# A top-1 mixture of low-rank experts: fp32 products taken directly instead of as three products of rounded parts, with TensorE's work per tile in another order

## What is computed

```python
h = h + _L0_ffn_ref(_layernorm(h, axis=-1), L0_ffn_route_w, L0_ffn_A, L0_ffn_Bw)

def _L0_ffn_ref(x, route_w, A, Bw):            # x (16, 128, 1024); A (8, 16, 1024); Bw (8, 1024, 16)
    logits = jnp.einsum('bsd,ed->bse', x, route_w)
    topk_v, topk_idx = jax.lax.top_k(logits, 1)
    route_weight = jax.nn.one_hot(topk_idx[..., 0], E, dtype=logits.dtype) * topk_v
    h = jnp.einsum('bsd,erd->bser', x, A)
    wh = route_weight[..., None] * h
    out = jnp.einsum('bser,eor->bso', wh, Bw) * SCALING
    return out
```

## Time and profile before

| what | value |
|---|---|
| median of 3 runs | 3199.29 us |
| the three runs | 3191.82, 12855.53 and 3199.29 us |
| span of the profiled execution | 3196.4 us |
| granted TensorE clock, mean over the span | 0.956 of full |
| PE busy | 2877.8 us, 90% of the span |
| DVE, ACT and POOL busy | 1687.9, 998.1 and 1014.7 us |

### The profile page before, as it was taken

One profiled execution on the slowest core, in us unless ns is written; L12 is line 12 of the kernel. 1 busy time (PEld: TensorE's weight loads), 2 busy tenths in 40 slices (PEclk: granted clock), 3 DMA queues, 4 the chain that ended last, 5 costly groups with the idle time before them and its releaser, 6 DMA issues. The chain is left out here.

```text
span 3196.4 us, 38209 instructions
## 1 busy us (share of the span) xinstructions
PE 2877.8 (90%) x13385; PEld 2335.5 (73%) x13385; DVE 1687.9 (53%) x2915; ACT 998.1 (31%) x2062; POOL 1014.7 (32%) x442
## 2 busy tenths in 40 slices
PE   6777499999989999998999999999999878649999
PEld 5555377777777777777777777777777667538888
DVE  5999654554544454455454446555444547662332
ACT  3443332333232333223332223333322323541111
POOL 3443233343333343333343333344333300141110
PEclk9999699999999999999999999999999979779999
DMA  4221032232222232222232222223222110110000
GB/s 93 47 49 40 28 93 73 74 95 74 78 66 73 72 94 78 76 75 66 67 92 85 72 74 72 66 86 92 72 72 72 60 53 1 40 60 27 27 26 27
DMA packets 55368, 206.90 MB, mean 65 GB/s; under 512 B 6880, under 2 KB 7136, under 8 KB 53216
## 3 DMA queue, kind: packets, MB, share of 16 engines
q1 hardware_dynamic: 55264, 205.52, 21.5%
HBM read 197.11 MB, written 8.39 MB: 64 GB/s over the span
## 5 line engine op out<-in xcount | busy, mean ns | idle before, releaser
L741 POOL TENSOR_TENSOR at_wlo<-at_wstage,at_whi 128x1024 fp32r<-128x1024 f32 x192 | 478.0, 2490 | 1374.9 <-ACT at_whi L764 1374.9
L1006 PE MATMUL at_proj<-qr_xhi,at_whi 128*128 128x512 f32 x1536 | 636.9, 415 | 57.5 <-POOL at_wlo L741 53.2
L1008 PE MATMUL at_proj<-qr_xhi,at_wlo 128*128 128x512 f32 x1536 | 612.4, 399 | 0.0
L1007 PE MATMUL at_proj<-qr_xlo,at_whi 128*128 128x512 f32 x1536 | 611.1, 398 | 0.0
L1006 PEld LDWEIGHTS at_proj<-qr_xhi,at_whi 128*128 128x128 f32 x1536 | 291.7, 190 | 135.0 <-issue 53.3
L1007 PEld LDWEIGHTS at_proj<-qr_xlo,at_whi 128*128 128x128 f32 x1536 | 291.6, 190 | 70.6 <-issue 7.4
L1008 PEld LDWEIGHTS at_proj<-qr_xhi,at_wlo 128*128 128x128 f32 x1536 | 290.9, 189 | 70.2
L733 POOL TENSOR_TENSOR at_wolo<-at_ostage,at_wohi 128x1024 fp32r<-128x1024 f32 x126 | 312.3, 2499 | 33.6 <-ACT at_wohi L770 33.5
L1054 PE MATMUL at_out<-at_wohi,at_ohi 128*128 128x512 f32 x1008 | 314.6, 394 | 9.0 <-DVE at_wolo L733 7.0
L1054 PE MATMUL at_out<-at_wohi,at_olo 128*128 128x512 f32 x1008 | 313.5, 393 | 0.0
L1054 PE MATMUL at_out<-at_wolo,at_ohi 128*128 128x512 f32 x1008 | 312.3, 391 | 0.0
(11 more groups left out here) (262 smaller groups left out, 4798.2 us busy)
## 6 DMA issues: line engine op xcount, KB each, us to landing
at_wstage<-in_w_qkv_dram SPq DMA_DIRECT2D x192, 512.0 KB, 3.6
at_ostage<-in_w_o_dram SPq DMA_DIRECT2D x128, 512.0 KB, 3.9
cv_x<-in_x_dram SPq DMA_DIRECT2D x32, 512.0 KB, 6.5
out_dram<-h SPq DMA_DIRECT2D x16, 512.0 KB, 2.6
fn_w_lo_raw<-in_w_t_dram SPq DMA_DIRECT2D x8, 512.0 KB, 7.0
fn_qka_lo_raw<-in_qka_t_dram SPq DMA_DIRECT2D x5, 512.0 KB, 5.9
sc_fhi_raw<-in_dft_fwd_dram SPq DMA_DIRECT2D x4, 512.0 KB, 7.4
sc_chi_raw<-in_lag_cos_dram SPq DMA_DIRECT2D x2, 512.0 KB, 9.7
```

What stands on the lines that cost most here:

```text
L741: pool.tensor_tensor(w_lo[j % 2][:, :], w_stage.buffers[j % 2][:, :], w_hi[j % 2][:, :].bitcast(F32), ALU.subtract).then_inc(wlo_done, 1)
L1006: pe.matmul(proj[:, j % 2, :], hi[:, w], x_hi[:, k, :], start=(k == 0), stop=False)
L1007: pe.matmul(proj[:, j % 2, :], hi[:, w], x_lo[:, k, :], start=False, stop=False)
L1008: last = pe.matmul(proj[:, j % 2, :], lo[:, w], x_hi[:, k, :], start=False, stop=(k == KT - 1))
```

## The change

In the mixture, and nowhere else:

- The rows `mx_x` and the weights `mx_ar`, `mx_b` and `mx_wt` stay plain fp32. The remainders are gone, with the operations on ACT and DVE that made the parts. Each projection block is one plain fp32 matmul instead of three fp32r ones (8 a tile instead of 24), and so is each output bank (2 instead of 6).
- `mx_ar` comes in one DMA of 1088 columns instead of 1024 and 64, and no operation follows it. PE waits for `mx_ar` and `mx_b` themselves.
- The transposed weighted values have two buffers `mx_wt0` and `mx_wt1`.
- PE's order in the turn of tile t is now: projections of t, transposes of t+1, outputs of t-1, transpose of `mx_wh` of t.

The core of the diff:

```diff
+    def copy(self, act, t, par, used, count):
+
+        after(act, self.turned, t + 1)
+        after(act, used, count)
+        act.copy(self.x[par][:, :, :], self.tp[:, :, :].rearrange("p a (k t) -> p (a k) t", t=P))\
+           .then_inc(self.hi_done, 1)
...
                 def before():
-                    ar.high(act)
                     rows.normalize(act, 0, 0)
-                    rows.high(act, 0, 0, pj_done, 0)
+                    rows.copy(act, 0, 0, pj_done, 0)
                     rows.normalize(act, 0, 1)
-                    b.high(act)
...
                     after(act, wt_mm, t + 1)
-                    after(act, out_mm, t)
-                    act.copy(wt_hi[:, :], wt[:, 0:P]).then_inc(wthi_done, 1)
+                    if not early(t, 2):
+                        after(act, out_mm, t - 1)
+                    act.copy(wt_sb[i % 2][:, :], wt[:, 0:P]).then_inc(wt_done, 1)
...
                 def body(g, i, t, on):
-                    if on(1):
-                        rows.low(dve, t + 1, (i + 1) % 2)
                     route_of(t)
                     if on(-1):
                         add(t - 1)
-                    after(dve, wthi_done, t + 1)
-                    dve.tensor_tensor(wt_lo[:, :], wt[:, 0:P], wt_hi[:, :].bitcast(F32), ALU.subtract)\
-                       .then_inc(wtlo_done, 1)
...
-                def outputs(t):
-                    after(pe, wtlo_done, t + 1)
+                def outputs(t, par):
+                    after(pe, wt_done, t + 1)
                     after(pe, added, t)
                     for c in range(2):
-                        w = slice(c * BANK, (c + 1) * BANK)
-                        pe.matmul(out[:, c, :], wt_hi[:, :], b.hi[:, w], start=True, stop=False)
-                        pe.matmul(out[:, c, :], wt_hi[:, :], b.lo[:, w], start=False, stop=False)
-                        mm = pe.matmul(out[:, c, :], wt_lo[:, :], b.hi[:, w], start=False, stop=True)
+                        mm = pe.matmul(out[:, c, :], wt_sb[par][:, :], b[:, c * BANK:(c + 1) * BANK],
+                                       start=True, stop=True)
                     mm.then_inc(out_mm, 1)
...
                 def body(g, i, t, on):
-                    after(pe, rows.lo_done, t + 1)
+                    after(pe, rows.hi_done, t + 1)
+                    after(pe, wh_done, t)
+                    for k in range(KT):
+                        mm = pe.matmul(pj[:, 0:ROUTED], rows.x[i % 2][:, k, :], ar[:, k * ROUTED:(k + 1) * ROUTED],
+                                       start=(k == 0), stop=(k == KT - 1))
+                    mm.then_inc(pj_done, 1)
                     if on(1):
                         rows.turn(pe, t + 1)
-
-                    after(pe, wh_done, t)
-                    xh, xl = rows.x_hi[i % 2], rows.x_lo[i % 2]
-                    for k in range(KT):
-                        w = slice(k * ROUTED, (k + 1) * ROUTED)
-                        pe.matmul(pj[:, 0:ROUTED], xh[:, k, :], ar.hi[:, w], start=(k == 0), stop=False)
-                        pe.matmul(pj[:, 0:ROUTED], xh[:, k, :], ar.lo[:, w], start=False, stop=False)
-                        mm = pe.matmul(pj[:, 0:ROUTED], xl[:, k, :], ar.hi[:, w], start=False, stop=(k == KT - 1))
-                    mm.then_inc(pj_done, 1)
                     if on(-1):
-                        outputs(t - 1)
+                        if early(t, 2):
+                            pe.wait_ge(b_in, 16)
+                        outputs(t - 1, (i + 1) % 2)
                     after(pe, wh_done, t + 1)
-                    after(pe, wtlo_done, t)
+                    after(pe, wt_done, t)
                     pe.transpose(wt[:, 0:P], wh[:, :], ident[:, :]).then_inc(wt_mm, 1)
```

More of the change, by code:

```diff
@@ L1105, with __init__ @@
     LINKS = 3 + RSQRT_LINKS + 1
-    def __init__(self, nc, ctx, name, h, ident):
+    def __init__(self, nc, ctx, name, h, ident, split=True):
         def sb(n, shape, dt=F32):
@@ L1115, in __init__ @@
         self.xn = sb("xn", [P, L])
-        self.x_hi = [sb(f"xhi{i}", [P, KT, P], F32R) for i in range(2)]
-        self.x_lo = [sb(f"xlo{i}", [P, KT, P], F32R) for i in range(2)]
+        if split:
+            self.x_hi = [sb(f"xhi{i}", [P, KT, P], F32R) for i in range(2)]
+            self.x_lo = [sb(f"xlo{i}", [P, KT, P], F32R) for i in range(2)]
+        else:
+            self.x = [sb(f"x{i}", [P, KT, P]) for i in range(2)]
         self.st = sb("st", [P, GROUP, 2, 6])
@@ L1206, in __init__ @@
     def __init__(self, nc, ctx, name, h, ident, rstd, shift):
-        super().__init__(nc, ctx, name, h, ident)
+        super().__init__(nc, ctx, name, h, ident, split=False)
         self.all_rstd, self.all_shift = rstd, shift
@@ L1226, in normalize, with turn @@
                        scale=self.all_rstd[:, bass.ds(t, 1)]).then_inc(self.normed, 1)
+    def turn(self, pe, t):
+        after(pe, self.normed, t + 1)
+        after(pe, self.hi_done, t)
+        for k in range(KT):
+            last = pe.transpose(self.tp[:, k // 4, (k % 4) * P:(k % 4 + 1) * P],
+                                self.xn[:, k * P:(k + 1) * P], self.ident[:, :])
+        last.then_inc(self.turned, 1)
+    def copy(self, act, t, par, used, count):
[3 more added lines that the diff above has]
+           .then_inc(self.hi_done, 1)
 class Weight:
@@ L1344, in sem @@
             return ctx.enter_context(nc.semaphore(name))
-        ar = Weight(nc, ctx, "mx_ar", a_route).add_high(nc, ctx)
-        b = Weight(nc, ctx, "mx_b", bw).add_high(nc, ctx)
+        ar = sb("mx_ar", [P, KT * ROUTED])
+        b = sb("mx_b", [P, L])
         rows = RowsAhead(nc, ctx, "mx", h, ident, rstd, shift)
@@ L1355, in mixture_stage @@
         wh = sb("mx_wh", [P, ER])
-        wt_hi = sb("mx_wthi", [P, P], F32R)
-        wt_lo = sb("mx_wtlo", [P, P], F32R)
+        wt_sb = [sb(f"mx_wt{i}", [P, P]) for i in range(2)]
         pj = ctx.enter_context(nc.psum_tensor("mx_pj", [P, BANK], F32))
@@ L1370, in _ @@
             def _(sp):
-                ar.load(sp)
+                sp.dma_start(ar[:, :], a_route).then_inc(ar_in, 16)
                 sp.dma_start(numbers[:, :], experts).then_inc(numbers_in, 16)
-                b.load(sp)
+                sp.dma_start(b[:, :], bw).then_inc(b_in, 16)
                 tables.load(sp)
@@ L1401, in before @@
                 def before():
-                    ar.low(dve)
-                    rows.low(dve, 0, 0)
-                    b.low(dve)
                     dve.wait_ge(numbers_in, 16)
```

13 lines of the change are left out of this document (7 added, 6 removed).

## The result

The median after is 3164.8 us (four runs, 3160.3 to 3167.7), against 3200.3 us for the kernel before beside it. That median is of four runs, of which one took 12855.53 us; the median of the other three is 3199.3. The ratio, without that run, is 0.9898, with a 95% interval of 0.9881 to 0.9916, so the change gains 1.0%. Between the medians that is 34.5 us without the long run; a later group of runs of both kernels gave 31.1 (3164.06 against 3195.12). The forecast was 3170 us, with 3158 to 3188 as its range.

The account below looks back on a forecast made before the run. Only the 121.8 us mixture, PE pacing its steady tiles, was taken to change in the 3196.4 us span; 17.7 + 10.2 - 0.3 = 27.6 us gives span 3168.8, median about 3170, range 3158 to 3188.

Parts of the forecast that it names:

- The start: Mixture's start: tile 0 normalized at once, weight casts and waits gone, first projection at 2601.6 instead of 2611.23, 9.6 us earlier.
- The price of plain fp32: Mixture matmuls, priced from attention rows: projections fall from 2.71 to 1.89 us a tile, outputs rise from 1.45 to 1.72.
- The count of passes: Projections by the skill's four passes for true fp32: eight blocks from 1.53 to 2.05 us, costing 0.5 us a tile.
- Tiles 0 to 4: Up to tile 4's mx_wh transpose: 17.7 us earlier, start's 9.6 included, with PE's stall of 3.1 us staying.
- the choice of 7: Early tiles: full clock assumed 7 us after the first projection, between no wait and the rows' 11.2 and 16.7.
- Tile 4 to the last projection: Steady tiles of 4.62 us: this stretch falls from 62.85 to 52.7 us, a gain of 10.2, between 8.6 and 13.7.
- The fall of the clock: After tile 4's wait: the clock falls again, half clock costing 3.5 us, with ends of 0 and 5.1.
- The tail: DVE's end of the mixture: outputs 0.5 us later, less 0.2 for mx_wtlo, so 0.3 us lost.
- The clock comes back late: Rival, 25%: the half clock lasts as before in the stage; gain only 22 us, 3176 us.
- No fall after tile 4: Rival, 7%: the clock stays up behind tile 4's stall; gain 31 us, 3167 us.
- The copy paces the tile: Rival, 8%: ACT or the mx_x copy paces tiles at 5.3 us, losing 10 us of gain; 3181 us.
- Slower through weight loads: Rival, 3%: plain fp32 weight loads do not overlap products, 61 us more, 34 slower than before; 3232 us.

Follow-up runs that it names:

- 68-column runs: Each projection matmul of 136 columns cut into two of 68, in both kernels: before 3263.54 us, stage 191.0; after 3203.08 us, stage 123.7.
- before twice: The kernel before, unchanged, in its first trace (stage 121.8 us) and run again (3200.26 us, stage 121.9).
- early statistics: DVE's statistics and chain for the last four tiles moved to the stage's start, in both kernels: before 3193.86 us, stage 114.4; after 3163.43 us, stage 85.9.
- order of after: Kernel after with projections again as three rounded products of parts, outputs plain, new order kept: 3202.2 us, ratio 1.0024, stage 123.3 us.
- early start: Kernel before with tile 0 normalized ahead of the mx_ar cast and PE waiting for weights only at first use: 3191.26 us, ratio 0.9989, stage 115.1 us.
- after twice: The kernel after, unchanged, in its first trace (3164.8 us, stage 89.2) and run again (3164.06 us, stage 91.1).
- split outputs: Kernel after with outputs again as three rounded products of parts, projections plain: 3161.6 us, ratio 0.9906, stage 86.6 us.
- both last versions: Kernel after with split outputs, early statistics, screen statistics spread: 3170.45 us, stage 96.2; with mx_b's remainder moved behind tile 0's weighting: 3157.82 us, stage 82.1.
- old order: Kernel after with PE's old order, transposes of t+1 ahead of projections of t: 3165.63 us, ratio 0.9918, stage 94.8 us.

## Why the prediction was right, step by step

**The start** (9.6 us forecast, 9.65 measured). Every step came as listed. The first of the waits explains about half: with the parts kept and only the waits moved, 5.1 us came.

**The price of plain fp32** (0.236 us a block forecast, 1.85 / 8 = 0.231 measured; outputs 1.72 forecast and measured). Taking the attention's 128-column row, scaled by columns, was right. The remark that rounded products do not scale with columns was right too, and the 68-column runs give the reason, which I did not have: a record of a projection costs no less than 0.11 us. At 136 columns rounding buys nothing, since three products at the least price cost more (0.339) than two plain records at 0.116. By the columns of the wide rows they would have cost 0.19. The count of passes that the prediction takes from the Trainium skill (FP8 and Floating Point Precision, section TensorE Precision Notes) points the right way where the columns set the price, at 512, and the wrong way at 136.

**Tiles 0 to 4** (17.7 us forecast with the start, 17.7 measured). The stall stayed, with 3.08 us for 3.1 forecast. The full clock came 6.0 us after the first projection, where I had chosen 7. PE waited for tile 1's copy until 2601.60, which is 6.8 us after its first projection, and any rise up to there gives the same sum. So the exact time cost nothing, and the choice of 7, for which there was no rule, was a lucky one.

**Tile 4 to the last projection** (10.2 forecast, 14.7 measured) is where the sum was mis-sized, in three terms. The fall of the clock, for which I took 3.5 us, cost 0 in the first trace and 1.7 in the second, and in both less than its 5.1 before. This is the largest of the three, and I had no rule for it. The turns of the loop, 1.0, cost nothing that shows: PE was busy for 43.00 of 43 us. And a tile took 4.56 us, not 4.62, which makes 0.6 over ten. That is 5.1 together. The last `mx_logits` gave back 0.4 us, because DVE was still at the statistics (a row of 0.68 us from 2670.64) when the last projections were done: it starts 2.43 us after them, where a steady tile has 2.06.

**The tail** (0.3 lost forecast, 0.3 gained measured). It was too small to argue about.

**The rivals.** *The clock comes back late* falls, and the reason is of use. I had put both slow rises of the rows down to the stage; the runs tie them to the way in which the projections are cut. It is not rounding as such, since plain products of 68 columns are as slow. From the first projection to the full clock, in all traces:

| projections | us to the full clock |
|---|---|
| 24 rounded matmuls of 136 columns (before twice, early statistics, order of after) | 16.7, 16.6, 16.8, 16.6 |
| the same, early start | 11.6 |
| 48 rounded matmuls of 68 columns | 27.0 |
| 8 plain matmuls of 136 columns (after twice, split outputs, early statistics, both last versions) | 6.0, 5.9, 6.0, 5.5, 5.9, 6.0 |
| the same, old order | 3.3 |
| 16 plain matmuls of 68 columns | 19.6 |

The starts differ in how long PE waits between tile 0's transposes and its first projection. Counted from those transposes, all seven traces with plain products of 136 columns have 8.6 to 9.3 us, the old order with them, and the others 19.3 to 35.

The falls behind tile 4 go the same way. After waits of 3.3 us the rounded kernels ran at the half clock for 10.2 us in all three (before twice, early start). The plain ones, after 2.7 to 3.2 us, had 0, 3.4, 0 (split outputs) and 3.4 (old order). Two kernels had a fall of 6.8 us after a shorter wait: the split projections in the new order (1.85 us) and the plain ones of 68 columns (1.41 us). So the length of the wait alone does not settle it.

The change thus gains a second time through the clock: by the mean granted clock, 0.83 over the 121.8 us before, some 41 us of the stage were at the half clock, and 11 after (14 in its second trace). Each costs half of itself where PE paces the stage. Why a stream of narrow products is slow to bring the clock back stays open.

*No fall after tile 4* was worked out at 31 us and is what the first trace shows (32.6); the second lies between it and the forecast. At 7% it was priced too low: two of four traces with such a wait and plain products of 136 columns have no fall. *The copy paces the tile* did not happen: PE had no gap. But it is what the split projections brought in this order. *Slower through weight loads* did not happen either, and the loads of plain fp32 are no slower than those of the parts (ns, minimum/median/maximum; the rounded projections of the kernel before, then the plain ones of the kernel after):

```profile
L1474 PEld LDWEIGHTS mx_pj<-mx_ar_hi,mx_xhi x128: 187/192/338, 2611.2 to 2709.8; 128*128 128x128 f32 x128
L1476 PEld LDWEIGHTS mx_pj<-mx_ar,mx_x x256: 186/190/338, 2594.8 to 2670.4; 128*128 128x128 f32 x128
```

Both lie under the products. So what the prediction expected of plain against split weights from the fast load does not show here.

**The time itself.** The span forecast was 3168.8. The stage came out 5.0 below that, the part ahead of it 6.8 below and the part behind it 1.4 above, which gives 3158.4. The runs vary by that much by themselves, and the median was 5 us below the forecast. That it came so near is in part luck, since the stage gained 32.6 us where the sum had 27.6. The 2% that the prediction names as the least that a measurement can tell is too coarse: the interval of the ratio is 0.9881 to 0.9916, so a gain of 1.0% stands clear of no change.

## What to carry to other kernels

Before splitting an fp32 product into rounded ones, read what each costs from start to start at its own width: here three rounded products win at 512 columns (1.48 against 1.72 us) and lose at 136 (2.71 against 1.85), since a record has a least price of 0.11 us; by an estimate the two meet near 200 columns. Dropping the parts pays a second time where they stand in a chain, at the start of a stage and between transposes and products, and an order that is good without them can be bad with them (new order against old: 89.2 us against 94.8 with plain projections, 123.3 against 121.8 with their parts). And where PE waits for an engine that is at work on something needed only later, that work is to be moved to where the engine is idle, after a look at what will then run beside it.

## What the runs showed of the hardware

- A record of a matmul with 128 rows, each with its own weight load, costs some 0.11 us at the full clock however narrow it is here: 0.11 for 68, 0.113 for 136 and 0.119 for 256 columns rounded, 0.110 for 68 and 0.116 for 136 plain. (The transposes, of 128 columns, take 0.10 to 0.11.) At the half clock 68 columns cost 0.21.
- The clock can fall with PE busy (at 2667.0 in the 68-column kernel, 5 us after a wait of 1.00 us). And the same wait of 3.08 us brought a fall of 3.4 us in one trace and none in another of the same kernel, so one trace doesn't settle what a wait costs in clock. Waits of 1.85 and 1.41 us in kernels with narrower or more products brought falls of 6.8 us.
- Small DVE operations on [128, 4] took 0.94 to 0.99 us instead of 0.16 or 0.17, one beside each of GpSimd's casts of about 1.0 us. Not every operation did: beside such casts in the kernel after, `MAX8` and `FIND_INDEX8` took 0.17 and 0.16 us, and the scaling of `mx_weight` 0.69 instead of 0.29. The Trainium skill, SBUF — State Buffer, section SBUF: two separate sides, says that the two engines share a pair of ports, and that a DVE operation in a two-port mode or with two SBUF inputs, or the GpSimd operation, whichever starts first, holds it for the whole instruction while the other blocks. The rows agree for the three slowed operations with two inputs or more; whether the other three ran in such a mode, no run here shows.
